# Windowed attention: 64x64 score tiles with the query norm folded into the exponential, keys ahead of queries

## What is computed

```python
h = shift_token(x)                              # upper 64 features come from the token before
q, k, v = split(h @ wqkv)                       # 8 heads of 64, per token
q = l2norm(q) * qs;  k = l2norm(k) * ksc
q, k = rotary_xpos(q, k)                        # cos/sin per token, xpos scale
# windows of 64 queries against 128 keys: the window before and the window itself
sim = (8 * q) @ k^T, with keys outside i-64 <= j <= i masked out
o = softmax(sim) @ v
x = x + o @ wo
h = layernorm(shift_token(x)) @ w1 + b1;  a, g = split(h)
x = x + (a * gelu(g)) @ w2 + b2
```

## Time and profile before

| | |
|---|---|
| median of 3 runs | 1347.29 us (1346.38 to 1348.74) |
| the profiled execution | 1350.65 us |
| its span, first to last instruction | 1348.1 us |
| PE busy / DVE / ACT / POOL | 86% / 77% / 68% / 35% of the span |
| TensorE's granted clock, mean | 0.944 of full speed |

### The profile page before, as it was taken

The page is one execution under the profiler, slowest core; times in us unless marked ns, Lnnn a source line. Parts: engine busy times, 40 slices in busy tenths (PEclk is TensorE's granted clock), DMA queues, the critical chain, the costliest instruction groups (busy, mean ns, idle before and its releaser), DMA issues. The chain is left out here.

```text
span 1348.1 us, 22359 instructions
## 1 busy us (share of the span) xinstructions
PE 1154.4 (86%) x6968; PEld 641.4 (48%) x6968; DVE 1031.8 (77%) x2065; ACT 918.6 (68%) x2746; POOL 472.6 (35%) x526
## 2 busy tenths in 40 slices
PE   4688888898888689988988998988998898899997
PEld 3233333233232137646635745744763663574573
DVE  5988889888987886687588678568758758857864
ACT  0588898897888657757646756755775764675673
POOL 2000000000000257257236536425635723653750
PEclk9699899998998979998998999988998999999999
DMA  5542241341330001101101101100110100110110
GB/s 182 160 125 63 63 126 39 86 117 33 100 109 16 0 0 29 29 0 28 29 9 36 29 1 28 29 9 8 33 25 1 40 17 16 28 29 1 29 29 16
DMA packets 24538, 58.90 MB, mean 44 GB/s; under 512 B 2736, under 2 KB 2928, under 8 KB 23280
## 3 DMA queue, kind: packets, MB, share of 16 engines
q1 hardware_dynamic: 24432, 57.62, 15.3%
HBM read 23.98 MB, written 18.87 MB: 32 GB/s over the span
## 5 line engine op out<-in xcount | busy, mean ns | idle before, releaser
L546 ACT ACTIVATE E<-slot,neg_max 128x512 f32<-128x512 f32 x512 | 343.9, 731 | 78.8 <-DVE neg_max L833 72.1
L833 DVE TENSOR_REDUCE neg_max<-slot 128x2 f32<-128x1024 f32 x256 | 305.9, 1211 | 42.4 <-PE slot L1087 42.3
L1087 PE MATMUL slot<-v_rows,k_rows 128*128 128x512 f32 x512 | 215.1, 491 | 62.0 <-ACT E L546 50.6
L463 POOL TENSOR_TENSOR work<-work,rot_work 128x512 f32<-128x512 f32 x128 | 162.3, 1269 | 205.6 <-DVE rot_work L868 204.6
L608 ACT ACTIVATE rot_work<-bank,neg 128x128 f32<-128x128 f32 x512 | 180.8, 374 | 67.1 <-DVE neg L895 30.4
L1135 PE MATMUL bank<-wqkv_sb,hs 128*128 128x512 f32 x384 | 200.7, 652 | 19.9 <-DVE rot_work L868 8.0
L1087 PEld LDWEIGHTS slot<-v_rows,k_rows 128*128 128x128 f32 x512 | 93.0, 199 | 246.9 <-ACT E L546 207.5
L477 POOL TENSOR_TENSOR rot_work<-rot_work,rz 128x512 f32<-128x512 f32 x128 | 133.3, 1043 | 189.6 <-DVE rz L900 189.2
L455 POOL TENSOR_TENSOR qz<-qT,rz 128x32 f32<-128x32 f32 x128 | 30.6, 239 | 418.7 <-DVE rz L837 418.7
L1097 PE MATMUL o_bank<-E,qz 128*32 128x512 f32 x1024 | 144.4, 638 | 1.7 <-POOL qz L455 1.7
L1153 PEld LDWEIGHTS bank<-kT,q_bd 128*128 128x128 f32 x1024 | 137.5, 195 | 8.9 <-issue 4.6
(11 more groups left out here) (122 smaller groups left out, 1750.2 us busy)
## 6 DMA issues: line engine op xcount, KB each, us to landing
v_rows<-v_scr SPq DMA_DIRECT2D x8, 1024.0 KB, 6.4
k_rows<-k_scr SPq DMA_DIRECT2D x32, 256.0 KB, 7.5
work<-v_al SPq DMA_DIRECT2D x16, 512.0 KB, 4.4
work<-v_al SPq DMA_DIRECT2D x16, 384.0 KB, 5.7
k_scr<-hi SPq DMA_DIRECT2D x16, 256.0 KB, 3.0
k_scr<-lo SPq DMA_DIRECT2D x16, 256.0 KB, 3.3
v_scr<-hi SPq DMA_DIRECT2D x16, 256.0 KB, 3.1
v_scr<-lo SPq DMA_DIRECT2D x16, 256.0 KB, 3.4
```

The source lines that it names most:

```text
L463: pool.tensor_tensor(qk[s][:, i, w, :], qk[s][:, i, w, :], sinp[s][:, n % 2, :], ALU.add).then_inc(rot_sum[s], 1)
L546: act.activation(E[:, g % E_RING, 2 * half + m, :], slot[:, m], ACT.Exp, bias=neg_max[:, n, m:m + 1], accum_out=z[:, n, m:m + 1]).then_inc ...
L833: dve.tensor_reduce(neg_max[:, n, :], slot[:], AX.X, ALU.max, negate=True).then_inc(max_ready, 1)
L1087: last = pe.matmul(bank, k_rows[:, hh, q, P * j:P * (j + 1)], v_rows[:, par, q, :], start=True, stop=True)
```

## The change

It changes the second stage alone, in five ways.

1. **Score tiles.** A unit is now one head with all eight windows: row 64c + t of a bank is query t of window 2m + c, and column block m holds its 128 keys. Scores are made for a pair of heads at a time, in two banks. Weights are 64x64 blocks of a plain transposed query `qT2`; head h uses partitions 64h to 64h + 63 of the array's rows, and window parity c goes to output partitions 64c to 64c + 63. The mask takes four 64-row matmuls of 512 columns per pair instead of two of 128 rows; the scores take 16 matmuls of 64x64 by 128 columns instead of 8 of 128x128 by 128 columns.
2. **Query norm.** Queries are no longer scaled by POOL. The row maximum is taken of unscaled scores (`top2`), DVE multiplies it by 1/|q| for two heads at once (128x8) into the bias `neg2`, and 1/|q| is the per-row `scale` of the exponential.
3. **Keys first.** Projections come as k, v of each tile and then the four q; the rotations take the four keys first. Clip, logarithm, exponential and Newton step are done for the keys and for the queries apart (128x32 each), and POOL scales the four key tiles between the rotary additions of the queries.
4. **Whole-bank copies.** A query tile is copied by ACT alone, 128x512. The value product of a pair fills one bank, and DVE copies it in one 128x512 instruction. `q_bd`, its clearing and its DVE copy are gone. `pr` and `prT` get four slots (three and two before).
5. **Order.** A new string for each engine. A stream has 94 PE steps per batch instead of 110. Stream x now starts first: its x2T, its 12 projections and its first query and key transposes come before or among y's first steps. At the end of the PE string 18 steps of y follow x's last one (from the transposes of y's unit 4 on); before, 8 steps of x followed y's last one.

The core of the diff (the new strings, the renamed semaphores and the generators that walk the steps are left out):

```diff
         for i in range(J):
-            out += [("q", l, i), ("k", l, i), ("v", l, i)]
+            out += [("k", l, i), ("v", l, i)]
+        out += [("q", l, i) for i in range(J)]
         for i in range(J):
             out += [("qT", l, i), ("kT", l, i)]
         for n in range(NU + AV_LAG):
-            for name, lag in (("sim", 0), ("pT", PT_LAG), ("av", AV_LAG)):
-                if 0 <= n - lag < NU:
-                    out.append((name, l, n - lag))
+            if n < NU and n % 2 == 0:
+                out += [("sim", l, n), ("sim", l, n + 1)]
+            if 0 <= n - PT_LAG < NU:
+                out.append(("pT", l, n - PT_LAG))
+            if n >= AV_LAG and (n - AV_LAG) % 2:
+                out.append(("av", l, (n - AV_LAG) // 2))
...
-        q_bd = each("q_bd", [P, PAIRS, NW, 2, W])
-        neg2, z2, rz2 = (each(n, [P, NU, 4]) for n in ("neg2_", "z2_", "rz2_"))
-        prT = each("prT", [P, 2, 4, P])
+        qT2 = each("qT2_", [P, PAIRS, T])
+        top2, neg2, z2, rz2 = (each(n, [P, NU, 4]) for n in ("top2_", "neg2_", "z2_", "rz2_"))
+        prT = each("prT", [P, PT_SLOTS, 4, P])
...
+            def b_scale(s, k, l, i):
+                if i == 0:
+                    pool.wait_ge(rn_ready[s], (k * L + l) * 2 + 1)
+                passed(pool, rot_sum[s], (k * L + l) * 2 * J + i + 1)
+                v = qk[s][:, i, 1].rearrange("p (h d) -> p h d", h=H)
+                pool.tensor_tensor(v, v, rn[s][:, i, 1, :].unsqueeze(2).broadcast_to([P, H, DH]),
+                                   ALU.mult).then_inc(k_ready[s], 1)
...
-            for s in range(STREAMS):
-                pool.memset(q_bd[s][:], 0.0).then_inc(s_qbd, 1)
...
+                bank, free = b_see(act, s, k, ("qT", l, i))
+                act.activation(qT2[s][:, :, P * i:P * i + P], bank[:].rearrange("p (c t) -> p c t", c=PAIRS),
+                               ACT.Copy).then_inc(free, 1)
...
-                act.wait_ge(max2[s], (k * L + l) * NU + u + 1)
+                act.wait_ge(bias2[s], (k * L + l) * PAIRS + u // 2 + 1)
                 if u >= PR_SLOTS:
                     b_see(act, s, k, ("pT", l, u - PR_SLOTS))
                 for w in range(4):
                     last = act.activation(pr[s][:, u % PR_SLOTS, w, :], bank[:, 2 * W * w:2 * W * (w + 1)], ACT.Exp,
-                                          bias=neg2[s][:, u, w:w + 1], accum_out=z2[s][:, u, w:w + 1])
+                                          scale=rn[s][:, w, 0, u:u + 1], bias=neg2[s][:, u, w:w + 1], accum_out=z2[s][:, u, w:w + 1])
...
+            def b_norm(s, k, l, w):
+                passed(dve, ss_ready[s], (k * L + l) * 2 * J + J * (2 - w))
+                v = ss[s][:, :, w, :]
+                dve.tensor_scalar(v, v, NORM_MIN2, SHIFT2, ALU.max, ALU.mult).then_inc(ss_all[s], 1)
+
+            def b_rnorm(s, k, l, w):
+                dve.wait_ge(ss_rsqrt[s], (k * L + l) * 2 + 2 - w)
+                newton(ss[s][:, :, w, :], rn[s][:, :, w, :], nt[s][:, :, w, :], b_link_of(s, k)).then_inc(rn_ready[s], 1)
...
+            def b_max(s, k, l, p):
+                for u in (2 * p, 2 * p + 1):
+                    bank, _ = b_see(dve, s, k, ("sim", l, u))
+                    last = dve.tensor_reduce(top2[s][:, u, :], bank[:].rearrange("p (w n) -> p w n", w=4), AX.X, ALU.max,
+                                             negate=True)
+                b_link_of(s, k)(last)
+                if p == 0:
+                    dve.wait_ge(rn_ready[s], (k * L + l + 1) * 2)
+                dve.tensor_tensor(neg2[s][:, 2 * p:2 * p + 2, :], top2[s][:, 2 * p:2 * p + 2, :],
+                                  rn[s][:, :, 0, 2 * p:2 * p + 2].rearrange("p m h -> p h m"),
+                                  ALU.mult).then_inc(bias2[s], 1)
...
+            def b_heads_out(s, k, l, p):
+                bank, free = b_see(dve, s, k, ("av", l, p))
+                dve.tensor_copy(oT[s][:, p, :], bank[:]).then_inc(free, 1)
...
-            def b_scores(s, k, l, u):
-                p, g = AT_UNITS[u]
-                tiles = [(t, l, 2 * g + i) for t in ("qT", "kT") for i in range(2)] if u < 2 else []
-                bank, full = b_take(pe, s, k, ("sim", l, u), *tiles)
-                pe.matmul(bank[:], ident_h[:], mask[:, 2 * W * g:2 * W * (g + 4)],
-                          start=True, stop=False)
-                for w in range(4):
-                    n = 4 * g + w
-                    last = pe.matmul(bank[:, 2 * W * w:2 * W * (w + 1)], q_bd[s][:, p, n].rearrange("p h t -> p (h t)"),
-                                     kT[s][:, p, W * n:W * n + 2 * W], start=False, stop=(w == 3))
-                last.then_inc(full, 1)
+            def b_scores(s, k, l, p):
+                tiles = [(t, l, i) for t in ("qT", "kT") for i in range(J)] if p == 0 else []
+                bank, full = zip(*(b_take(pe, s, k, ("sim", l, 2 * p + h), *tiles) for h in range(2)))
+                for h in range(2):
+                    r = slice(W * h, W * h + W)
+                    for c in range(2):
+                        pe.matmul(bank[h][W * c:W * c + W, :], ident_h[r, r], mask[r, 2 * W * c:2 * W * (c + 4)],
+                                  start=True, stop=False)
+                for m in range(J):
+                    for h in range(2):
+                        r = slice(W * h, W * h + W)
+                        for c in range(2):
+                            n = 2 * m + c
+                            last = pe.matmul(bank[h][W * c:W * c + W, 2 * W * m:2 * W * (m + 1)],
+                                             qT2[s][r, p, W * n:W * (n + 1)], kT[s][r, p, W * n:W * (n + 2)],
+                                             start=False, stop=(m == J - 1))
+                        if m == J - 1:
+                            last.then_inc(full[h], 1)
...
+                bank, full = b_take(pe, s, k, ("av", l, p), ("pT", l, 2 * p), ("pT", l, 2 * p + 1))
+                for n in range(NW):
                     v = v_al[s][:, n // 2] if n % 2 else v_sh[s][:, n // 2]
                     for h in range(2):
-                        last = pe.matmul(bank[W * h:W * h + W, W * w:W * (w + 1)],
+                        last = pe.matmul(bank[W * h:W * h + W, W * n:W * (n + 1)],
                                          v[:, P * p + DH * h:P * p + DH * (h + 1)],
-                                         prT[s][:, u % 2, w, W * h:W * (h + 1)], start=True, stop=True)
```

More of the change, by code:

```diff
@@ L52 @@
 B_BANKS = 4
-AT_UNITS = [(p, g) for p in range(PAIRS) for g in range(2)]
-NU = len(AT_UNITS)
+NU = H
 PT_LAG, AV_LAG = 2, 3
-PR_SLOTS = 3
+PR_SLOTS = 4
+ROTATIONS = [(i, w) for w in (1, 0) for i in range(J)]
+PT_SLOTS = 4
 LN_CHAIN = 2 + 3
-B_CHAIN = LN_CHAIN + (2 + LN_CHAIN) * L
+B_CHAIN = LN_CHAIN + (2 * 2 + PAIRS + LN_CHAIN) * L
 def bank_uses():
@@ L90 @@
[L90 to L93, removed]
+        "xxxxxxxxxxxxxyxxyyxyxyxxxyxyxxyyyyxxyxxxyxyxxxyyxyxxxyxyxyyxyyxyxxyxxyxxyxyyxxxyyyxxxxyxxxyyyxyxyxxx"
@@ L488, in b_stream @@
                             yield
-                        for n in range(2 * J):
-                            b_scale(s, now[s], l, n)
-                            yield
+                            if n >= J:
+                                b_scale(s, now[s], l, n - J)
+                                yield
                         for u in range(NU):
@@ L974, in b_stream @@
                                 yield
-                            if u >= AV_LAG:
-                                b_heads_out(s, now[s], l, u - AV_LAG)
+                            if u >= AV_LAG and (u - AV_LAG) % 2:
+                                b_heads_out(s, now[s], l, (u - AV_LAG) // 2)
                                 yield
@@ L1181, in b_project_out @@
                 for p in range(PAIRS):
-                    b_done(pe, s, k, *(("av", l, u) for u in range(NU) if AT_UNITS[u][0] == p))
+                    b_done(pe, s, k, ("av", l, p))
                     last = pe.matmul(bank[:], wo_sb[:, l, p, :], oT[s][:, p, :], start=(p == 0), stop=(p == PAIRS - 1))
@@ L1225, in b_stream @@
                         for i in range(J):
-                            for c in range(3):
+                            for c in (1, 2):
                                 b_project(s, now[s], l, i, c)
                                 yield
+                        for i in range(J):
+                            b_project(s, now[s], l, i, 0)
+                            yield
                         for i in range(J):
@@ L1233, in b_stream @@
                         for u in range(NU + AV_LAG):
-                            if u < NU:
-                                b_scores(s, now[s], l, u)
+                            if u < NU and u % 2 == 0:
+                                b_scores(s, now[s], l, u // 2)
                                 yield
@@ L1239, in b_stream @@
                                 yield
-                            if u >= AV_LAG:
-                                b_values(s, now[s], l, u - AV_LAG)
```

(2 more changed lines are left out.)

158 lines of the change are left out of this document (66 added, 92 removed).

## The result

The changed kernel takes 1360.78 us (median of 9 runs, 1355.4 to 1370.96) against 1348.87 us for the kernel before in the same rounds: a ratio of 1.0087, 95% interval 1.0063 to 1.0112. It is slower by about 12 us where 60 us less were forecast. The profiled execution took 1357.1 us.

What follows compares the result with a forecast made beforehand. PE, 89% busy in the second stage, was taken as the bound. Scores -59, clears -5, waits for `q_bd` -6, order +10 make -60: 1350.65 to 1290.7, less 3.4 gives 1287 us; range 1243 to 1328.

Steps and rivals of the forecast that it cites:

- Four quarters side by side: Second-stage score matmuls: four run together, a pair takes 1.28 us where two units took 2.20; -59 us of PE.
- The clears: Start of the second stage: without the two POOL clears of `q_bd`, DVE's held group is released; -5 us.
- DVE 36 us less against 25: DVE's busy time in the second stage: copies removed, small operations added; -25 taken, 0 beside PE's gain.
- POOL 72 less against 68: POOL in the second stage: half of 128 scalings go, 68 us of 132; nothing more taken off the total.
- The tail: End of the run: 36 us with one stream instead of 16, PE about half used in the added 20; 8 us.
- PE's time comes off the stage: Second stage: PE, 89% busy, is scarcest, so time taken off it should largely come off the stage; 59 us.
- it has 320 us free, so 0: Scale from memory in 512 exponentials: 0.02 to 0.085 us each, +11 to +44 us on ACT, counted as 0.
- The rival for the slower side: Pairs starve the exponentials: gaps of about 3 us, 144 us in all; 1373 us at 60% uncovered; chance 0.08.
- I gave them +10 us: New order strings: 8 us for the longer one-stream end, 2 for the start; +10 us, bounds 0 and 25.
- my lower bound: New DVE multiplication of 8 columns: between 0.27 us and 0.57 us each, +17 to +36 us for 64.
- The estimate of 26 us: Added small DVE operations wait for POOL over shared memory: 26 us of DVE, in the time-into-waits rival, chance 0.2.

Runs made afterwards that it cites:

- experiment 2: Changed kernel with every score matmul issued twice: 1400.7 us; in another kernel, the same score matmuls two quarters at a time instead of four: 1379.7 us.
- experiment 8: Changed kernel reordered with its third set of order strings, with every score matmul issued twice: 1339.9 us, against 1304.8 us without the doubling.
- experiment 1: Changed kernel, its own strings, with no scale from memory in the exponential and the bias product multiplying by ones: 1320.8 us against 1360.8.
- experiment 3: Kernel before the change, with a scale of one read from memory in each of its 512 exponentials: 1367.7 us, ratio 1.0123.
- experiment 6: Changed kernel, its own strings, with the bias made for each head by itself instead of for two heads at once: 1348.9 us.
- experiment 5: Changed kernel with no scale from memory in the exponential and with order strings made for the shorter exponential: 1281.4 us.
- the third strings: Changed kernel, its steps unchanged, with a third set of order strings made by search for its profiled durations: 1304.8 us, ratio 0.9719.

## Why the prediction was wrong

**What held.** Four quarters side by side (1.11 us a pair against the 1.28 taken; PE's busy time fell by 58 us against 59). The clears, -5.5 us against -5. DVE 36 us less against 25, POOL 72 less against 68. The tail: 39 us with one stream against 36.

**The step that failed first: "PE's time comes off the stage".** From 89% busy I read that nearly every microsecond of PE would show. Experiments 2 and 8 put it at 0.46 to 0.63. By that the 58 us of PE are worth 27 to 37 us, not 59. PE was the busiest engine, but the stage had 106 us of PE idle already. My reading is that these belonged to chains of one stream (scores, maxima, exponentials, sums, products, transposes), which did not get shorter by the same amount.

**A term that was missing: the clock.** The sum took the granted clock as it was. It fell from 0.95 to 0.93 in the second stage, and 15 of 64 score pairs ran partly at the lower level where 5 of 128 units had. At the full clock the scores alone would give (2.20 - 1.11) x 64 = 70 us of PE, an estimate from one pair of each; 58 were left.

**The step that cost most: "it has 320 us free, so 0".** The size was right: I bounded the scale at 0.02 to 0.085 us an exponential from a 512-column copy, and it is 0.086 to 0.089 (experiments 1 and 3). The whole 0.085 was the right reading, and scaling it down by the length was not: 85 ns there at 512 columns, 86 to 89 here at 128. The Trainium skill, ScalarE: Activation LUTs, section "What ACT_TABLE_LOAD costs", says about 93 ns for each operand that is read per partition; the trace agrees (86 to 89 ns), and I had not drawn on it. Wrong was to set the cost at zero for the free time of the engine. The exponentials stand four in a row for each unit between a stream's maxima and its sums, and 46 us less of them are 39.5 us less of time (experiment 1).

**The rival for the slower side had the wrong weight and the right place.** Its gap is in the timeline (2.55 us of ACT idle between two pairs), and it put PE's wait before the mask. Alone, it costs about 10 us (experiment 6) of the 144 it could; it needed the long exponentials and the strings beside it.

**The strings.** I gave them +10 us and counted their tail. Other ones are worth 56 us (1360.8 to 1304.8, the higher clock and a tail of 29 us instead of 39 included), against 6 us for the kernel before. The prediction could have seen that strings are the glue of such a kernel, but not from any row of the kernel before how well the new ones fit: that needed durations which only the new profile shows.

Together, in the second stage: 885.7 - 5.5 (clears) - 27 to 37 (PE at the measured share) + 39.5 (scale) = 883 to 893, and 896.7 was measured; the 4 to 14 left have the size of the pairs (about 10), with nothing over for the order and the clock. These parts overlap, so the sum is a check of sizes and no proof. With scale and misfit both gone the kernel takes 1281.4 us, where the sum without them had said 1287. Part of that agreement is luck, since the PE term was too large and the order's gain was not in it.

Open: which property of the strings that came with the change is the bad one. That they were made for a shorter exponential would fit, as the scale costs 40 us in them and 23 in the fitted ones; but without the scale too, other strings gain 39 us more (experiments 1 and 5), so this is not all. The tail is one candidate: x's last transposes stand 39 us before the end in experiment 1 and 16 in experiment 5, 23 of the 39. No run changed the tail alone. Open too is how much of each difference is the clock and how much brings the clock about.

## What to carry to other kernels

When the busiest engine is at 89% and the others at 50 to 70, with a few streams interleaved by hand, do not take the busiest engine for the bound. Free time on an engine does not make an addition to it free: price what lies in a stream's chain, on whichever engine. Here 46 us of ACT were worth 39.5, and of the time added to PE a half to two thirds reached the total. An operand read per partition instead of a constant cost ScalarE about 0.09 us per instruction at 128 and at 512 columns, so it is dear in short instructions. After a change of step sizes, make the hand-written order again for the new durations before judging the change: here that turned +0.9% into -2.8%. And look at the granted clock of each kernel that you compare: it moved with the strings here, and took part in the differences.

## What the runs showed of the hardware that I had not expected

- Four 64x64 float32 matmuls of 128 columns on the four quarters of the array cost what one costs at the full clock: 32 instructions end 1.07 us after the first starts, against 1.05 us for eight of 128x128. Two at a time (experiment 2) they take 1.54 us.
- Going from one form of tile to another is not free. In the kernel before, the instruction behind eight 128x128 score matmuls starts 0.16 us before the last of them has ended (724.85 + 1.05 against 725.74). Behind the quarter tiles the next full-size transpose starts only 0.07 us before (708.32 + 1.07 against 709.32). Start to start, from the last score matmul to the instruction behind it, that is 0.11 and 0.20 us, and the trace has the same two distances at the other places where PE goes on at once at the full clock. So this change of form holds PE for 0.09 us. It is no cost of the change as a whole: 128 value units stood between full-size matmuls before, and 64 value groups and 64 score pairs stand there now:

```profile
725.74 1.02 PE L1135 MATMUL bank<-wqkv_sb,hs 128*128 128x512 f32 x2
```

```profile
709.32 0.75 PE L1229 MATMUL bank<-ident,y 128*128 128x128 f32 x4
```

- The clip of the sums at half the width (128x32, L879) takes 785 ns where the full width took 653 (and 574 in the kernel with the third strings), while the new product with two inputs in memory (L897) takes 178 ns, under my lower bound. The first stands beside POOL's rotary additions in the new order. I take it that POOL holds it up, but this was not tested. The estimate of 26 us that the prediction worked out from the Trainium skill, SBUF — State Buffer, section "SBUF: two separate sides", for the added products did not show: DVE's busy time fell by 36 us, more than the 25 forecast without them.
